# An involution and mixture-of-experts block on one core: rims zeroed instead of whole images, first waits of ScalarE narrowed, tap weights taken in by piece, and eight adds on GpSimd for ten in tiles 2 to 7

## The reference, cut to what matters

```
x = x + conv(_ln_c(x))        # h = reduce_w.x + b; kern = span_w.h + b  (49 taps x 16 groups)
                              # out = (kern * patches).sum(over the 49 taps)
t = tokens(x)
t = t + ffn(_ln_t(t))         # softmax over 8 experts, top 2, silu(x.w1) * (x.w3), then w2
```

## Time and profile before

| | |
|---|---|
| median of 3 runs | 1503.39 us (1500.45 to 1503.68) |
| the profiled execution | 1498.94 us, of which the span of the core is 1497.1 us |
| PE, PEld busy | 1243.9 us (83%), 1015.6 us (68%) |
| DVE busy | 1122.8 us (75%) |
| POOL busy | 1112.2 us (74%) |
| ACT busy | 579.5 us (39%) |
| products on DVE, L851 | 592, 627.9 us |
| GpSimd's adds, L1084 and L1088 | 28 and 192, 62.9 and 435.9 us |
| PE's sums, L601 | 2864 matmuls of 128 x 128 |

### The profile page before, as it was taken

How to read it: one execution, slowest core, us unless ns; L and a number is a source line. 1 busy time by engine, 2 the same in 40 slices (tenths; PEclk the granted TensorE clock), 3 DMA queues, 4 the chain that set the end, 5 groups by cost and what they waited for, 6 DMA issues and landing times. The chain is left out here.

```text
span 1497.1 us, 23125 instructions
## 1 busy us (share of the span) xinstructions
PE 1243.9 (83%) x7667; PEld 1015.6 (68%) x7667; DVE 1122.8 (75%) x1663; ACT 579.5 (39%) x1960; POOL 1112.2 (74%) x788
## 2 busy tenths in 40 slices
PE   4898878788988989899899898899989887587771
PEld 2676767676766777677787777777778676465661
DVE  5998888988898998888889898888889943222220
ACT  4333333334443444444345343454434244133230
POOL 4787979784686887678788687877778875665665
PEclk9999898998999999999999999999999999899996
DMA  4111111112232242332324232243322445666652
GB/s 124 41 60 48 59 49 59 49 31 88 53 79 60 69 97 63 88 78 60 85 59 103 62 86 62 60 100 83 71 58 48 105 119 129 174 137 134 145 117 25
DMA packets 93346, 120.40 MB, mean 80 GB/s; under 512 B 11531, under 2 KB 72428, under 8 KB 93082
## 3 DMA queue, kind: packets, MB, share of 16 engines
q1 hardware_dynamic: 53802, 90.97, 20.0%
q0 software_dynamic: 39424, 27.96, 13.3%
HBM read 78.92 MB, written 42.65 MB: 81 GB/s over the span
## 5 line engine op out<-in xcount | busy, mean ns | idle before, releaser
L851 DVE TENSOR_TENSOR prod<-kern_ps,xn 128x896 f32<-128x896 f32 x592 | 627.9, 1082 | 65.7 <-PE kern_ps L586 63.2
L586 PE MATMUL kern_ps<-h_stack,span 98*128 98x448 f32 x1372 | 466.3, 426 | 112.7 <-DVE prod L851 72.1
L1088 POOL TENSOR_TENSOR acc_p<-acc_p,prod 128x896 f32<-128x896 f32 x192 | 435.9, 2270 | 74.1 <-DVE prod L851 69.4
L1109 POOL DMA_INDIRECT out<-y_tok,idx x224 | 351.6, 1570 | 137.4 <-issue 66.2
L601 PE MATMUL acc_ps<-ident_sb,prod 128*112 128x128 f32 x2864 | 388.4, 280 | 0.0
L601 PEld LDWEIGHTS acc_ps<-ident_sb,prod 128*112 128x112 f32 x2864 | 341.3, 137 | 37.9 <-DVE x L1053 7.8
L586 PEld LDWEIGHTS kern_ps<-h_stack,span 98*128 98x128 f32 x1372 | 227.1, 200 | 205.5 <-DVE prod L851 121.5
L1097 POOL DMA_INDIRECT xs<-rows_x,slots x224 | 219.0, 978 | 61.0 <-issue 41.3
L536 PEld LDWEIGHTS bank<-w2b,hid 114*128 114x128 f32 x1344 | 181.7, 202 | 50.7 <-DVE xf_lo L1046 26.0
L536 PE MATMUL bank<-w2b,hid 114*128 114x128 f32 x1344 | 190.1, 288 | 26.2 <-DVE xf_lo L1046 15.9
L780 ACT ACTIVATE silu<-h_ps 114x512 f32<-114x512 f32 x132 | 79.0, 598 | 235.0 <-PE h_ps L627 235.0
(11 more groups left out here) (154 smaller groups left out, 1349.9 us busy)
## 6 DMA issues: line engine op xcount, KB each, us to landing
wb<-wexp SPq DMA_DIRECT2D x56, 684.0 KB, 5.4
xb<-xs SPq DMA_DIRECT2D x56, 264.0 KB, 3.0
w2b<-in_w SPq DMA_DIRECT2D x56, 171.0 KB
xt<-in_x SPq DMA_DIRECT2D x28, 224.0 KB, 3.4
out<-x SPq DMA_DIRECT2D x28, 224.0 KB, 2.6
wexp<-wb SPq DMA_DIRECT2D x8, 684.0 KB, 3.2
xs<-rows_x,slots POOLq DMA_INDIRECT x224, 2.3
out<-y_tok,idx POOLq DMA_INDIRECT x224
```

The source lines that it names most:

```text
L586: last = mm(kern_ps[:, g % 2, i, 0:N], span[:, k * C:(k + 1) * C], h_stack[:, t % 2, :], start=True, stop=True)
L851: v.tensor_tensor(pair_rows(dst), kern.rearrange("p i (r w) -> p i r w", w=W), taps, ALU.mult).then_inc(s_prod, 1)
L1088: g_.tensor_tensor(acc_p[:], acc_p[:], prod[:, (t * TAPS + u) % PRING, :], ALU.add).then_inc(s_padd, 1)
L1109: g_.indirect_dma_start(out=out, out_offset=bass.IndirectOffsetOnAxis(ap=idx[:, b % XBRING, q:q + 1], axis=0), in_=y_tok[:, b % 2, q * C:( ...
```

## The change

- `BY_POOL` has nine units (0, 2, 5, 7, 10, 12, 15, 17, 20) for tiles 2 to 7 instead of eleven. GpSimd makes eight adds, and PE sums sixteen units instead of fourteen.
- GpSimd writes the three small constants first, and then zeroes only the rims of the two images: six memsets of 189, 55 x 6 and 189 columns for each image.
- ACT waits at the start for the small constants alone, and runs one small activation (`Square` on one column), which has the table load before it. The waits for the constants from DRAM and for DVE stand at the `h` of tile 0, the one for the rims at its `xn`. PE waits for the five constants and for three signals of DVE.
- The tap weights land in `rows_x` instead of `prod`, the first two pieces ahead of the last two small constants. ACT takes in pieces 0 to 4 before tile 0 and pieces 5 and 6 at steps 1 and 4 of it, DVE pieces 5 and 6 at steps 3 and 7; PE waits at each unit of tile 0 for the pieces that it reads. DVE's memset of the last columns of `rows_x` follows the last piece.

```diff
-BY_POOL = [tuple(range(0, 21, 2)) if t < LATE else tuple(range(0, 22, 3)) for t in range(TILES)]
+BY_POOL = [tuple(range(0, 21, 2)) if t < 2 else (0, 2, 5, 7, 10, 12, 15, 17, 20) if t < LATE else tuple(range(0, 22, 3)) for t in range(TILES)]
...
-PIECE_J = (3, 4, 5, 7, 8, 10, 12)
+
+PIECE_AT = [FIRST + j for j in (4, 4, 8, 10, 22)] + [1, 4]
+PIECE_LO_AT = [FIRST + j for j in (5, 5, 9, 11, 23)] + [3, 7]
...
@@ sync
-                    for dst, src in FIRST_CONSTS:
-                        sp.dma_start(dst, src).then_inc(s_const, 16)
                     for i in range(KS):
-                        sp.dma_start(prod[0:98, i, 0:SCOLS], w_span[:, i * SCOLS:(i + 1) * SCOLS]).then_inc(s_span_in[i], 16)
+                        if i == 0:
+                            for dst, src in FIRST_CONSTS[:3]:
+                                sp.dma_start(dst, src).then_inc(s_const, 16)
+                        if i == 2:
+                            for dst, src in FIRST_CONSTS[3:]:
+                                sp.dma_start(dst, src).then_inc(s_const, 16)
+                        sp.dma_start(raw_piece(i, 0), w_span[:, i * SCOLS:(i + 1) * SCOLS]).then_inc(s_span_in[i], 16)
...
@@ tensor
             pe.wait_ge(s_const, 16 * NCONST)
-            pe.wait_ge(s_setp, 2)
-            pe.wait_ge(s_setv, 4)
+            pe.wait_ge(s_setv, 3)
...
+                if t == 0:
+                    pe.wait_ge(s_piece_lo, min(2 * u + 1, KS * KS - 1) // KS + 1)
...
-                if S == 0:
-                    pe.wait_ge(s_piece_lo, KS)
...
@@ scalar
-            act.wait_ge(s_const, 16 * NCONST)
-            act.wait_ge(s_setp, 2)
-            act.wait_ge(s_setv, 4)
+
+            act.wait_ge(s_setp, 1)
+            act_f(veps["ln1"][:, 0:1], eps["ln1"][:], ACT.Square)
...
-                if p == -1 and j in PIECE_J:
-                    i = PIECE_J.index(j)
-                    act.wait_ge(s_span_in[i], 16)
-                    act_f(span[:, i * SCOLS:(i + 1) * SCOLS], prod[0:98, i, 0:SCOLS], ACT.Copy).then_inc(s_piece_hi, 1)
+                for i in range(KS):
+                    if S == PIECE_AT[i]:
+                        act.wait_ge(s_span_in[i], 16)
+                        act_f(span[:, i * SCOLS:(i + 1) * SCOLS], raw_piece(i, 0), ACT.Copy).then_inc(s_piece_hi, 1)
...
@@ vector
+                        v.tensor_tensor(hi, raw_piece(i, 64), hi.bitcast(F32), ALU.subtract).then_inc(s_piece_lo, 1)
+                        if i == KS - 1:
+                            dve.wait_ge(s_piece_lo, KS)
+                            v.memset(rows_x[:, :, :, :, C:ROW], 0.0)
...
@@ gpsimd
-            g_.memset(xn[:], 0.0).then_inc(s_setp, 1)
             g_.memset(minus_half[:], -0.5)
             g_.memset(eps["ln1"][:], LN_C_EPS)
             g_.memset(eps["ln2"][:], LN_T_EPS).then_inc(s_setp, 1)
+
+            for i in range(2):
+                image = xn[:, i * IMG:(i + 1) * IMG]
...
+            k.then_inc(s_setp, 1)
             pool.wait_ge(s_setp, 2)
```

More of the change, by code:

```diff
@@ L397, in bank_filled, with raw_piece @@
             return BANK_NO[use] + 1
+        def raw_piece(i, first):
+            last = 97 if first else 98
+            return rows_x[first:last].rearrange("p a b c d -> p (a b c d)")[:, i * SCOLS:(i + 1) * SCOLS]
         def xn_at(tile):
@@ L659, in bank_use @@
                 if name == "xn":
+                    if t == 0:
+                        act.wait_ge(s_setp, 2)
                     act_f(window(xn_at(t) + PAD * PW + PAD), rows(bank[:, 0:N]), ACT.Copy).then_inc(s_bank_out, 1)
                 elif name == "h":
+                    if t == 0:
+                        act.wait_ge(s_const, 16 * NCONST)
+                        act.wait_ge(s_setv, 3)
                     if t >= 2:
@@ L804, in _ @@
             v.memset(done[:], 0.0)
-            v.memset(rows_x[:, :, :, :, C:ROW], 0.0)
             v.memset(ones_bf[:], 1.0).then_inc(s_setv, 1)
@@ L812, in _ @@
             dve.wait_ge(s_setv, 4)
-            dve.wait_ge(s_setp, 2)
             def small(g, parts, start, stop):
@@ L1027, in _ @@
                 p, j = divmod(S, TAPS)
[L1028 to L1031, removed]
-                    v.tensor_tensor(hi, prod[64:97, i, 0:SCOLS], hi.bitcast(F32), ALU.subtract).then_inc(s_piece_lo, 1)
+                for i in range(KS):
+                    if S == PIECE_LO_AT[i]:
+                        dve.wait_ge(s_piece_hi, i + 1)
+                        hi = span[64:97, i * SCOLS:(i + 1) * SCOLS]
+                        v.tensor_tensor(hi, raw_piece(i, 64), hi.bitcast(F32), ALU.subtract).then_inc(s_piece_lo, 1)
+                        if i == KS - 1:
+                            dve.wait_ge(s_piece_lo, KS)
+                            v.memset(rows_x[:, :, :, :, C:ROW], 0.0)
                 if j == 16 and 0 <= p < WPIECES:
@@ L1066, in _ @@
             g_.memset(eps["ln2"][:], LN_T_EPS).then_inc(s_setp, 1)
+            for i in range(2):
+                image = xn[:, i * IMG:(i + 1) * IMG]
+                left, right = PAD * PW + PAD, (PAD + H - 1) * PW + PAD + W
+                g_.memset(image[:, 0:left], 0.0)
+                g_.memset(image[:, left + W:right].rearrange("p (r w) -> p r w", w=PW)[:, :, 0:2 * PAD], 0.0)
+                k = g_.memset(image[:, right:IMG], 0.0)
+            k.then_inc(s_setp, 1)
             pool.wait_ge(s_setp, 2)
```

## The result

The changed kernel takes 1479.71 us (median of four runs, 1478.88 to 1482.42) against 1503.54 for the kernel before: the ratio is 0.9847, with an interval of 0.9826 to 0.9867. That is 23.8 us by the medians; the two profiled executions, 1498.94 and 1478.88 us, differ by 20.1. The forecast was 1483.7, in a range of 1471 to 1495.

A forecast was written before the change was run, and what follows sets the result against it. The prediction took GpSimd, late at one place and nearly full, to bound tiles 3 to 7, and a chain of first waits the start. Terms 5.5 + 11.1 + 2.5 + 0.6 = 19.7 us off 1503.4 gave 1483.7, range 1471 to 1495.

The forecast's parts named there:

- The first product: Start: small constants first, fewer and covered copies; first product at 17.9 to 18.2 us instead of 25.42, 7.3 us earlier.
- Given back: Tile 0: moved low parts of pieces 5 and 6 and the memset cost 1.8 us, about half absorbed by waits.
- term A: Start: the earlier first product less what tile 0 gives back, 5.5 us less, between 2.5 and 7.5.
- B: Tiles 3 to 7: DVE's idle time falls to 3.15 us each, 11.1 us less in all, between 4 and 14.
- C: Tiles 3 to 7: DVE's busy time falls 0.5 us a tile, 2.5 us less, between 0 and 11.
- D: Tile 2 gains from the earlier power less the sums' cost, tile 8 starts with less left over: together 0.6 us less.
- The mechanism of B: Tiles 3 to 7: GpSimd's late second power delays PE's transposes, and the lower clock follows; one add fewer ahead cures it.
- the signs that were named: Tiles 3 to 7: ACT's shift waits below 1 us, PE's clock near 1.00, GpSimd idle before its first add.
- The price of a sum on PE: Tiles 2 to 7: each added sum costs DVE about 0.24 us where sums follow each other; about 0.5 us a tile.
- The clock: Tiles 3 to 6 at 33 to 35 us and tile 7 near 37, with PE's mean clock in them near 1.00.
- Kept to the end: From tile 8 on the order is unchanged, so what the early tiles win should be kept to the end.
- The rival "slower": Tiles 2 to 7: PE becomes the bound through twelve added sums; 1510 us or more, chance 0.04.

The follow-up runs named there:

- E5: Kernel before, with DVE's first low part waiting for GpSimd's first shift; one execution of 1501.15 us, first product at 23.85 us.
- e1: Kernel before with only the new split of GpSimd's adds in tiles 2 to 7 (eight adds); 1487.55 us, ratio 0.9911.
- e4: Kernel before with the rims and narrower first waits, all seven pieces still copied ahead of tile 0; 1497.13 us, ratio 0.9966.
- e6: Kernel after, with pieces 5 and 6 moved back ahead of tile 0; 1480.66 us, ratio 0.9853.
- e2: Kernel after with the old table (ten adds, four ahead of the second power), so the start alone; 1495.37 us, ratio 0.9952.
- e7: Kernel after with ten adds in tiles 2 to 7, three ahead of the second power, last at unit 21; 1484.64 us, ratio 0.9886.
- e8: Kernel after with eight adds in tiles 2 to 7, but four ahead of the second power; 1478.71 us, ratio 0.9855.
- e9: Kernel after with seven adds in tiles 2 to 7 and seventeen sums on PE; 1491.04 us, ratio 0.9947.
- e12: Kernel after with ten adds in tiles 2 to 7, three ahead of the second power, last at unit 20; 1488.39 us, ratio 0.9923.
- e10: Kernel after with ten adds, four ahead; experts' low part reads zeros from PSUM, so low parts are left out; 1485.47 us, ratio 0.9901.
- e11: Kernel after (eight adds); experts' low part reads zeros from PSUM, so low parts are left out; 1470.26 us, ratio 0.9799.
- e13: Kernel after, all computed: ACT copies the experts' high part to PSUM and DVE subtracts from there; 1471.05 us, ratio 0.9799.

## Why the prediction held, point by point

**The first product, 7.3 us earlier forecast, 8.84 measured.** ACT's first statistics start at 3.52 (3.7 forecast). The chain from there is 13.1 us, not 14.2. What was sized wrong: the prediction took the pieces beside the power as covered and kept power and shift at their 3.0 us. Since DVE's low parts no longer stand beside them, they take 1.04 and 0.20 us, and ACT's normalisation starts 1.43 us after the power does. E5 shows that cause by itself. The prediction set the sharing against the change only, for the moved pieces; it worked more strongly for it, at the power. It did not name what brought this about: the first two low parts stand right behind their pieces in DVE's queue, and the late `lower_sb` kept DVE from them until the shift was made.

**Given back, 1.8 us forecast.** In the two profiled executions it is 1.1 (8.84 less 7.7 at tile 0's tap), but that is one draw. From the first product to tile 0's tap are 30.9 us in the kernel before and 33.0 to 34.1 in e1, e4, e5 and e6, which have all pieces ahead of tile 0 as well; with two pieces among the products they are 32.0 in the kernel after, and 32.0 to 34.6 in e2, e7, e8, e9 and e12, whose tile 0 has the same instructions. So what the moved pieces cost can't be told from how tile 0 varies by itself, and the agreement with 1.8 is luck as much as anything. The moved low parts took 1.09 and 1.76 us; the first stretched an add of GpSimd to 3.00. The whole of term A was 5.5 by forecast and 6.6 by e2.

**Tiles, B + C + D: 14.2 us forecast.** From tile 1's tap to tile 8's the two profiled executions differ by 15.9, e1 gives 14.4 for the whole kernel. By parts: DVE's idle time in tiles 3 to 7 fell by 12.6 (B, 11.1), its busy time by 2.2 (C, 2.5), tile 2 shrank by 0.7. The experts' low parts alone fell by 4.9 us (16.0 to 11.1); other instructions of DVE took some of it back, and which was not looked into.

**The mechanism of B is half right.** Some of the signs that were named came: no wait of PE at the second norm's transposes, ACT's wait at 1.6 us a tile instead of 4.1 (under 1 was forecast, though power and shift alone are 1.3). Others did not: the clock is not near 1.00 in all of these tiles, and GpSimd has no idle time before its first add of tile 4. And e8 is as fast as the kernel after without the first two, so they were no proof. The step that failed is "GpSimd bounds these tiles by being late at one place", with the pause at the transposes as what it costs. That B came within 1.5 us of its size does not confirm the working behind it.

What the runs show in its place is the number of adds. With four adds ahead of the power, ten against eight are 18.2 us of the section (e2, e8); with three ahead they are 7.5 (e7, the kernel after). The prediction had the reason in the same paragraph, as its second: GpSimd's own work, 68.3 us for two tiles. With ten adds it is a floor that these tiles come close to. Tiles 3 and 4 together took 75.7 us (before), 71.7 (e7), 73.1 (e10) and 70.0 (e12), tiles 5 and 6 took 75.2, 71.4, 71.3 and 70.6. Before its first add of tile 5 GpSimd waits 7.05 us for PE in the kernel before, 5.29 in e10, 3.44 in e7 and 1.66 in e12. So the kernel before stands 7 us a pair above that floor, there are only these 7 to win while ten adds stay, and e12 has won most of them. Two cures that have little in common, the earlier power and the low part from PSUM, each bring 8 us of the section with ten adds.

How far the sum alone explains the rest stays open. The two cures were not run together with ten adds, which would show whether the pairs stop at 68.3 us. A pair above that number is no proof by itself: in e8, with eight adds, 8.5 us less work and 8.4 us of waiting on GpSimd, tiles 3 and 4 took 68.9. The pair took 67.5 us in the kernel after and 64.3 in e11. And of the 7.5 and 6.7 us by which e7 and e12 are slower than the kernel after, 2.2 and 3.7 lie in tile 2, where GpSimd is busy for only 24 of 34 to 35 us. E2, with ten adds as well, takes 32.4 for that tile, so there it is the order of adds and sums and not their number. Why the place of the power stops mattering with eight adds stays open too: in e8 the tiles also had short low parts (1.2 to 1.4 us in tiles 3 to 7), so the two are not apart there.

**The price of a sum on PE** was given as 0.24 us each, up to 0.5. It can't be read from the pair that was moved. With the third the tiles are 1.75 us longer on average (e9), of which a part is the low part's, as said above. No run shows the estimate right, and e9 shows that it can't be carried on to the next sum.

**The clock.** The prediction asked for near 1.00 in all of these tiles. It is 1.00 in tile 4, 0.95 in tiles 3 and 6, and 0.90 and 0.91 in tiles 5 and 7. The pause at the transposes is neither needed for a fall nor enough for a low mean: the kernel after has no such pause in these tiles, and e8, with pauses of 1.5 to 1.8 us in tiles 3 to 6, has 1.00, 0.95, 1.00, 0.95 and 1.00 in tiles 3 to 7. With the low part from PSUM, e11 has 1.00 in tiles 3, 4 and 6, and e13 in tiles 3 to 6.

**Kept to the end.** Nearly: 2.7 of 23.7 us went in tile 9, where the kernel after spent more time at the lower clock. That tile took 45.1 to 45.6 us in the kernel before, e2, e9 and e10, 46.8 to 48.1 in the kernel after, e1, e4 to e8 and e12, and 43.2 and 42.6 in e11 and e13. The old and the new start are in both of the first groups, and so is the table with ten adds as before; the table of the change, with eight adds and the low part from SBUF, is in the second group alone (the kernel after, e1, e6). E4 and e5 lose as much with the old table, so the loss doesn't need it; whether it favours the loss, and what decides it, stays open.

**The rival "slower"** did not come, but one step more goes its way: with seven adds the section is 10.5 us longer than with eight. Whether PE is the bound there was not shown.

## What to carry to other kernels

If an engine looks late at one place, add up its work over a whole period before you move the late instruction: here moving it brought 8 us, with the engine nearly full after it, and taking work off brought 18. That a foretold sign appears proves little: here a run had the whole effect without it. And an instruction of DVE with two operands in SBUF beside a busy GpSimd is worth a detour: reading one of them from PSUM cost ACT 0.9 us a tile and brought 8.7 us (e13).

## What was not expected of the hardware

- One tensor_tensor of DVE with both inputs in SBUF, 128x684, took 0.85 us at best and up to 3.41 where GpSimd's adds and DMAs alternate; with one input in PSUM 0.84 to 0.86, in all eight tiles of two kernels (e10, e11). The stretch works both ways: the low parts took GpSimd's power from 1.04 to 1.79 us and its shift of 112x4 from 0.20 to 1.08.
- DVE's small casts and copies (112x112, 112x8), one input each, took 2.2 to 2.3 us beside GpSimd's memset of 7688 columns (the kernel before), ending less than 0.3 us after it, and 0.16 to 0.23 without it (the kernel after).
- The kernel before and e1 have the same instructions in tile 0, and PE's times agree up to 33.6 us. There they part by one spell of PE's lower clock (1.04 against 1.84 us for eight transposes), and tile 0 ends 3.2 us later in e1.
